# 3x3 pass: the activated rows are kept sorted by column phase, and put back in order where they are added to x

## What is computed

```python
y = relu(_conv(_gn(x), ds_w3[0], ds_b3[0], pad=1))    # 3x3, 64 -> 64 channels
y = _conv1x1(y, ds_w1[0], ds_b1[0])
# att(y): 16 channels go through a 13x13 filter, 48 (f_idt) go straight on
out = jnp.concatenate([out_lk + out_dk, f_idt], axis=1)
return _conv1x1(_conv1x1(out, fus_w, fus_b), fin_w, fin_b)
# levels 1 to 3: the same on x averaged over 2x2, 4x4 and 8x8, repeated to full size and added
x = x + ...
```

## Time and profile before

| | us |
|---|---|
| median of 3 runs | 3250.32 (3243.36 to 3251.4) |
| the profiled execution | 3247.2 |
| its span, first to last instruction | 3245.1 |
| the 3x3 pass in it, unit products from about 1190 to 1875 us | 685 |
| granted TensorE clock, mean over the span | 0.916 |

### The profile page before, as it was taken

How to read it: one execution, slowest core, us unless ns; L and a number is a source line. 1 busy time by engine, 2 the same in 40 slices (tenths; PEclk the granted TensorE clock), 3 DMA queues, 4 the chain that set the end, 5 groups by cost and what they waited for, 6 DMA issues and landing times. The chain is left out here.

```text
span 3245.1 us, 39970 instructions
## 1 busy us (share of the span) xinstructions
PE 2823.2 (87%) x12454; PEld 2270.3 (70%) x12454; DVE 2182.8 (67%) x3100; ACT 878.2 (27%) x1534; POOL 642.0 (20%) x699
## 2 busy tenths in 40 slices
PE   0599999996999959999999948989996599999998
PEld 0476666665888748888888836767775477777777
DVE  7444444423344367777777767888877799999998
ACT  1111111111000025555555522222210333333332
POOL 5534443312111034344343300000000000000000
PEclk9999999997766769999999969999997799999999
DMA  4322222200000068888888722343334233333332
GB/s 83 97 70 67 68 67 67 67 13 22 8 10 9 3 118 199 196 192 195 188 199 193 165 83 82 130 149 132 120 132 161 109 110 93 100 110 110 98 95 80
DMA packets 288980, 339.86 MB, mean 105 GB/s; under 512 B 24848, under 2 KB 243856, under 8 KB 274576
## 3 DMA queue, kind: packets, MB, share of 16 engines
q1 hardware_dynamic: 285360, 338.12, 38.7%
q10 hardware_dynamic: 3552, 0.89, 0.2%
HBM read 212.58 MB, written 123.60 MB: 104 GB/s over the span
## 5 line engine op out<-in xcount | busy, mean ns | idle before, releaser
L373 PE MATMUL ps_all<-vh,u_h 128*128 128x512 f32 x960 | 383.1, 399 | 42.5 <-DVE vl L2568 42.5
L375 PE MATMUL ps_all<-vh,u_l 128*128 128x512 f32 x960 | 383.1, 399 | 0.0
L374 PE MATMUL ps_all<-vl,u_h 128*128 128x512 f32 x960 | 382.7, 399 | 0.0
L373 PE MATMUL ps_all<-vh,t_h 128*128 128x512 f32 x576 | 231.2, 401 | 35.4 <-DVE vl L1612 34.9
L2488 ACT ACTIVATE vh<-rt,gn 128x528 fp32r<-128x528 f32 x192 | 130.6, 727 | 442.1 <-DVE rt L2545 286.2
L373 PEld LDWEIGHTS ps_all<-vh,u_h 128*128 128x128 f32 x960 | 180.8, 188 | 90.0 <-issue 42.9
L375 PE MATMUL ps_all<-vh,t_l 128*128 128x512 f32 x576 | 230.0, 399 | 0.0
L374 PE MATMUL ps_all<-vl,t_h 128*128 128x512 f32 x576 | 229.1, 398 | 0.0
L374 PEld LDWEIGHTS ps_all<-vl,u_h 128*128 128x128 f32 x960 | 181.0, 188 | 46.4
L375 PEld LDWEIGHTS ps_all<-vh,u_l 128*128 128x128 f32 x960 | 180.8, 188 | 46.2
L373 PE MATMUL ps_all<-ch,w_h 128*128 128x512 f32 x280 | 125.2, 447 | 86.8 <-ACT cc L1938 52.3
(11 more groups left out here) (373 smaller groups left out, 6781.4 us busy)
## 6 DMA issues: line engine op xcount, KB each, us to landing
xc<-in_x SPq DMA_DIRECT2D x128, 256.0 KB, 3.9
xr<-in_x SPq DMA_DIRECT2D x128, 256.0 KB, 4.1
x_layer<-xr SPq DMA_DIRECT2D x64, 512.0 KB, 2.7
xq<-x_layer SPq DMA_DIRECT2D x32, 1024.0 KB, 4.9
x_layer<-xq SPq DMA_DIRECT2D x32, 1024.0 KB, 3.9
out<-ot SPq DMA_DIRECT2D x64, 512.0 KB, 5.3
xw<-in_x SPq DMA_DIRECT2D x112, 288.0 KB, 4.8
xw<-x_layer SPq DMA_DIRECT2D x16, 1152.0 KB, 8.7
```

The costliest lines, as they stand in the source:

```text
L373: pe.matmul(o, wh, xh, start=first, stop=False, skip_group_check=True)
L374: pe.matmul(o, wh, xl, start=False, stop=False, skip_group_check=True)
L375: return pe.matmul(o, wl, xh, start=False, stop=last, skip_group_check=True)
```

## The change

The layout of `rf`, `rh` and `rl` becomes (phase, row, column / 4) with four phases. ScalarE does the sorting: both `relu` activations read `yt` at a distance of four elements (16 bytes) and write rows of 32. The attention product then reads adjacent elements. The identity product keeps the sorted order in PSUM, and `add_x` undoes it: it reads and writes `xr` four elements apart. `add_x` becomes a plain sum, since the bias `bz` is added in `plain` of the level-1 pass instead. The second `relu` write waits for `q_f` >= n, the attention product of the unit before, where it waited for the identity products of two units back.

```diff
                     def plain(i, k):
-                        dve.tensor_copy(z1[:, 8 * k:8 * k + 8, :].rearrange("p a b -> p (a b)"),
-                                        ps_q[:, u % 2, :]).then_inc(qfree, 1)
+                        dve.tensor_scalar(z1[:, 8 * k:8 * k + 8, :].rearrange("p a b -> p (a b)"), ps_q[:, u % 2, :],
+                                          bz[:, 0:1], None, ALU.add).then_inc(qfree, 1)
-            rf = sb("rf0", [P, 8, W], stack=st)
-            rh = sb("rh0", [P, 2, 8, W + 8], F32R, stack=st)
-            rl = sb("rl0", [P, 2, 8, W + 8], F32R, stack=st)
+            rf = sb("rf0", [P, 4, 8, 32], stack=st)
+            rh = sb("rh0", [P, 2, 4, 8, 36], F32R, stack=st)
+            rl = sb("rl0", [P, 2, 4, 8, 36], F32R, stack=st)
...
-                        act.activation(rf[:, :, :], yt[:, :, :], ACT.Relu, bias=b3p[:, 0:1],
+                        y = yt[:, :, :].rearrange("p n (q d) -> p d n q", d=4)
+                        act.activation(rf[:, :, :, :], y, ACT.Relu, bias=b3p[:, 0:1],
                                        accum_out=rs[:, bass.ds(i, 1), t]).then_inc(r_f, 1)
-                        act.wait_ge(q_x, 2 * n + 2)
-                        act.activation(rh[:, t % 2, :, 2:2 + W], yt[:, :, :], ACT.Relu,
-                                       bias=b3p[:, 0:1]).then_inc(r_h, 1)
+                        act.wait_ge(q_f, n)
+                        act.activation(rh[:, t % 2, :, :, 1:33], y, ACT.Relu, bias=b3p[:, 0:1]).then_inc(r_h, 1)
...
-                        dve.tensor_tensor(rl[:, t % 2, :, 2:2 + W], rf[:, :, :], rh[:, t % 2, :, 2:2 + W].bitcast(F32),
+                        dve.tensor_tensor(rl[:, t % 2, :, :, 1:33], rf[:, :, :, :], rh[:, t % 2, :, :, 1:33].bitcast(F32),
                                           ALU.subtract).then_inc(r_l, 1)
...
-                            v = xr[:, t % NS, 4 * h:4 * h + 4, :].rearrange("p a b -> p (a b)")
-                            dve.scalar_tensor_tensor(v, ps_all[:, 6 + h, :], bz[:, 0:1], v, ALU.add,
-                                                     ALU.add).then_inc(x_o, 1)
+                            v = xr[:, t % NS, :, :].rearrange("p n (q d) -> p d n q", d=4)[:, 2 * h:2 * h + 2, :, :]
+                            dve.tensor_tensor(v, ps_all[:, 6 + h, :].rearrange("p (d n q) -> p d n q", d=2, q=32), v,
+                                              ALU.add).then_inc(x_o, 1)
...
-                            v = (slice(None), s, slice(4 * h, 4 * h + 4), slice(2, 2 + W))
-                            product(pe, ps_all[:, 6 + h, :].rearrange("p (a b) -> p a b", b=W), idt0_h[:, :],
+                            v = (slice(None), s, slice(2 * h, 2 * h + 2), slice(None), slice(1, 33))
+                            product(pe, ps_all[:, 6 + h, :].rearrange("p (d n q) -> p d n q", d=2, q=32), idt0_h[:, :],
                                     idt0_l[:, :], rh[v], rl[v], True, True).then_inc(q_x, 1)
                         for dc in range(4):
-                            v = (slice(None), s, slice(None), slice(dc, dc + 133, 4))
+                            q0 = dc // 2
+                            v = (slice(None), s, (dc + 2) % 4, slice(None), slice(q0, q0 + 34))
```

More of the change, by code:

```diff
@@ L1377, in _ @@
                         pool.memset(ft[:, :, :, :], 0.0).then_inc(b_p, 1)
-                        for t in (rh, rl, vh, vl):
+                        for t in (vh, vl):
                             pool.memset(t[:, :, :, :].bitcast(F32), 0.0).then_inc(b_p, 1)
+                        for t in (rh, rl):
+                            pool.memset(t[:, :, :, :, :].bitcast(F32), 0.0).then_inc(b_p, 1)
                         pool.memset(zrow[:, :], 0.0).then_inc(b_p, 1)
```

## The result

| | before | after |
|---|---|---|
| median, us | 3247.87 (3242.76 to 3251.4) | 3254.26 (3245.05 to 3275.87) |
| ratio to before | | 1.0027, 95% interval 1.0017 to 1.0037 |
| the profiled execution, its span | 3247.2, 3245.1 | 3253.2, 3251.0 |
| granted TensorE clock, mean | 0.916 | 0.915 |

Slower, as forecast, but by 6 us and not by 33. The spread of the runs has grown from 9 to 31 us.

What follows compares the result with a forecast made beforehand. The ScalarE and VectorE loop was to replace TensorE as bound: 8.4 + 2.10 + 0.72 = 11.2 us for 10.75, +30 us over 63 units, +3 at the ends, 3280 us. Own range 3250 to 3305, overall range 3195 to 3330.

Steps and rivals of the forecast that it cites:

- What bounds: 3x3 pass: TensorE, the bound at 10.75 us per unit, gives way to a ScalarE and VectorE loop of 11.2.
- The prices: 3x3 pass, per unit: two activations reading at 16 bytes cost 2.10 us more, sums into x 0.72 more.
- Wait and bias: rh's wait for the previous unit's attention product and the bias moved to level 1: both taken as costing nothing.
- the 2 KB pattern: Large-filter pass, ScalarE reading elements 2 KB apart: 1.03 ns more per element, carried over to the activations at 16 bytes.
- Rivals 1: 3x3 activations: ScalarE reads 16 bytes apart for free, TensorE stays the bound at 9.45 us, 3165 us; chance 0.14.
- rival 2: 3x3 activations: ScalarE pays only VectorE's 0.71 ns per element, loop 10.6 us, 3240 us; chance 0.11.
- 4 (an attention product that doesn't get faster): 3x3 pass: rows of 34 cost what the stride did, TensorE stays at 10.85 us, again 3280; 0.61 with the forecast.
- The base of the loop: 3x3 pass, yt b to next yt b without TensorE, before the change: steps sum to 8.42 us, 8.4 used.
- er about 1.61: VectorE's er in the loop of the 3x3 pass, start to start: 1.61 us, from its 1.70 less 0.1 overlap.
- if er moves off GpSimd's work: 3x3 pass: last sign that the forecast is wrong, as GpSimd's start hangs on the store after the moved sums.
- er with or without GpSimd beside it: VectorE's er in the 3x3 pass: 1.2 to 1.7 us, 0.3 us per unit either way, part of the own range.
- Rival 3, the clock: 3x3 pass: gaps drop TensorE to the 1.2 GHz level, 3395 us if in all units, 3330 in some; chance 0.10.

Runs made afterwards that it cites:

- GpSimd placed: Kernel after, with GpSimd's short sums made to run beside the sums into x and its long sum beside the second part of vl: 3238.28 us, 0.9973.
- the prices alone: Kernel before, with activations and sums into x at 16 bytes but the attention product still reading every fourth element: 3286.63 us, 1.0120.
- the last version: Kernel after, with the second activation reading the sorted rf and GpSimd's short and long sums held to fixed positions by waits: 3182.59 us, 0.9802.

## Why the prediction was right in sign and wrong in size

**What bounds.** Right in kind. TensorE hands over to the loop over ScalarE and VectorE; waits stand before rl and before the first 3x3 matmul, none before yt.

**The prices.** rf and rh 2.15 and 2.13 us where I took 2.20; yt b to rl is 5.27 for a forecast of 5.39. Sums into x 1.08 each as forecast, start to start 1.95 the pair for 2.04. Attention matmuls 0.131 for 0.1275, identity 0.255 as forecast (1.53 / 6). Wait and bias: nothing. Carrying the 2 KB pattern over to 16 bytes was sound to 0.07 us. Rivals 1 (no price on ScalarE), 2 (VectorE's price) and 4 (an attention product that doesn't get faster) fall with these rows. That rival 2's time of 3240, from a loop of 10.6, lies near what the kernel takes with GpSimd placed (3238) is chance: its price was wrong, and its loop was short for that reason and not for want of collisions.

**The base of the loop: the step that failed.** "er about 1.61 (its 1.70 less the 0.1 by which neighbours overlap)" went into the sum as what er costs in every unit; the means of er and cr, which gave 8.38, hold the same collisions. In that unit er, which starts at 1514.95, was 1.70 because a short sum of GpSimd stood in front of it until 1515.56. GpSimd in before:

```profile
1514.64 2.53 POOL L1506 TENSOR_TENSOR zr<-zr,z 128x256 f32<-128x256 f32 x2 [6.60 <-DMA xr<-in_x]
```

Over the pass er has two lengths there, not one with a spread (ns min/median/max): 26 of the 62 are 1.21 to 1.22 us, 35 are 1.69 or 1.70, and one is 3.17.

```profile
L1606 DVE TENSOR_TENSOR er<-xw x62: 1208/1692/3171, 1196.3 to 1848.9; 128x1024 f32<-128x1024 f32 x62
```

By itself er costs 1.23, start to start 1.14. A collision is a property of two phases, and the change moves both. So the loop of before without it is 8.42 - 0.47 = 7.95, and after's is 8.42 + 2.10 + 0.72 = 11.24, less 0.47 (er), 0.12 (activations) and 0.09 (sums): 10.56, which is what the undisturbed units and the run with GpSimd placed show. On top comes what GpSimd hits: nothing in 38 units, 0.2 to 2.4 us in 23, on average (679.4 - 18.4 for the two short ones) / 61 - 10.56 = 0.28.

So of the miss per unit 0.47 - 0.28 = 0.19 us is the collision, put in as a fixed part of er, and 0.21 the two sizes: about 12 us and 13 us over the pass. I had +30 for the full units and 61 x (10.84 - 10.76) = 5 were measured, 25 too many. With the 4.3 of the first yt b, and ends of +5.5 (short units 2.4, behind the last yt b 3.1) where I had 3, that is the 27 us between 3280 and the profiled 3253.2.

**The sign is in part luck.** The sum said that the loop is longer than TensorE's 10.75, collision or not. The loop without collisions is 10.56, shorter than that: by itself it takes 12 us from the 61 full units, and both runs without a hit in it, GpSimd left out and GpSimd placed, are faster than before (0.9963 and 0.9973). After is slower because collisions add 17 us to the full units, in a pattern that the sum didn't have. The prediction's last sign of being wrong, "if er moves off GpSimd's work", is what happened in 38 units.

**"er with or without GpSimd beside it (1.2 to 1.7 us, 0.3 us per unit either way)".** The doubt was named but priced from the wrong side. Without GpSimd the unit loses 0.47, and the other way there is no such cap: cr behind a running long sum costs 1.46 (units of 12.05), and er once took 3.15 in after (the unit of 12.91). The 3.17 in the row above is the same thing in before, in a unit of 10.76 like the others: the slack hid it.

**Rival 3, the clock.** The mechanism exists, but not where it would have decided. Of after's 58 gaps of TensorE over 0.5 us in this pass, ahead of 3x3 matmuls, two (2.24 and 2.21 us) were followed by matmuls 0.43 apart, for eight or nine of them; from 1300 to 1800 us the clock is 1.00. And such a drop costs no time by itself: the unit with the first one is 11.17 long, like its neighbours, because 8 x 0.19 = 1.5 us more of 3x3 still fits beside the loop.

**Why GpSimd leaves er in after and stays on it with the prices alone** is argued, not shown. GpSimd starts when its loads have landed (280.9 us of waiting for them in the 500), these are issued after the store, and the store after the sums into x: a loop of its own, whose time against the unit's sets the phase. No run held the landing and varied the unit. The wider spread of after's runs would fit that, if which units are hit differs from run to run (each kernel has one trace, so none shows it): with GpSimd's sums left out it is 3.6 us, and with fixed positions 6.1 and, in the last version, 1.1 us, all over fewer runs (6, 9 and 4 for 20).

## What to carry to other kernels

Before adding up a loop that is not the bound yet, take each operation at its undisturbed time, from the fastest of its kind, and write collisions as a term of their own with a price between nothing and the whole length of the other engine's instruction; slack hides them only as long as the bound stays where it is. When the loop becomes the bound, fixing where the other engine's work falls can be worth more than making it smaller: here 89 us lay between the worst and the best position of the same sums. And pay for a strided read once: the second reader takes the sorted copy.

## What the runs showed of the hardware

**One at a time, for a whole instruction.** Whichever of a GpSimd sum and one of VectorE's cr, er, vl and rl starts second waits for the other's end: vl 3.19 for 1.27 behind a long sum, cr 2.00 for 0.54, rl 1.76 for 1.23 behind a short sum. What it costs is what is left of the other, less 0.1 to 0.3 us: 2.11 left and 1.92 paid by that vl, 1.72 and 1.46 by cr, 0.37 and 0.23 by rl in the run whose sums wait for yt b. The other way round the long sum takes 3.13 for 2.14 when the second part of vl stands 0.19 ahead of it, at 1.31. yt and the sums into x, whose one operand is in PSUM, are as long beside a sum of GpSimd as without (yt 0.66 to 0.76 us against 0.66 to 0.74, a sum at 16 bytes 1.04 to 1.12 against 1.04 to 1.17, over the pass in all traces in which yt isn't sorted). The Trainium skill says so (SBUF — State Buffer, Who interferes with whom): GpSimd shares a port pair with VectorE, held for the whole instruction by whoever issues first, and a VectorE operation with two SBUF inputs contends with a GpSimd one that reads SBUF, one with a single SBUF input, outside its two-port modes, does not. The traces agree in both; cr has one SBUF input and is hit, and the page lists its kind, `tensor_scalar`, among those that can take both port pairs. Read against the earlier trace rows, that rule says where to look when er takes 1.70: at GpSimd's timeline.

**ScalarE at 16 bytes.** 2.13 us for 1024 elements, 1.10 to 1.15 adjacent: 0.96 ns more per element ((2.13 - 1.15) / 1024). TensorE's moving operand pays as well: 272 columns 0.245 us at 16 bytes, 0.131 in rows of 34. The Trainium skill's note on cachelines, named in the prediction, agrees with both.

**The clock's lower level, and what it didn't cost.** In the run with the long sum in front of cr TensorE stood still for 1.9 to 2.3 us in every second unit or so, and mostly fell to the lower level, 1.2 GHz, at its return or up to five matmuls later:

```profile
1554.95 0.79 PE L373 MATMUL ps_all<-vh,t_h 128*128 128x512 f32 x1 [2.31 <-DVE vl L1615]
1555.54 0.63 PE L374 MATMUL ps_all<-vl,t_h 128*128 128x512 f32 x1
1555.96 0.63 PE L375 MATMUL ps_all<-vh,t_l 128*128 128x512 f32 x1
```

0.43 apart for five more, then 0.23 again: 30 of its 61 gaps over 0.5 us ended so, and the granted clock is 0.93 from 1300 to 1800 us. Its units stay at 12.05 with and without: the slower matmuls take 1.5 us of standing still, so the gap of the next unit is only 0.8, and none of the gaps of 0.7 to 1.0 us in this run was followed by slow matmuls. The length of the gap alone does not decide: with the prices alone a gap of 0.71 us was followed by slow matmuls and one of 1.71 was not; in after one of 2.43 was not.
